# Moving the first expert group's preparation forward into the relu layer of a two-layer transformer kernel

## The reference

```python
x = x + L0_xattn(layernorm(x), ctx)
x = x + L0_ffn(layernorm(x))                    # 8 experts choose tokens, small attention inside
x = x + L1_xattn(layernorm(x), ctx, masks)      # self attention, cross attention, relu FFN
x = x + L1_ffn(layernorm(x))                    # 16 routed experts and 2 shared ones
```

```python
h = relu(y @ ff_w1 + ff_b1)                     # 128 -> 512
y = layernorm(y + h @ ff_w2 + ff_b2, g3, b3)    # divides by (std + EPS)
x = x + y
```

```python
xn = layernorm(x)
scores = sigmoid(xn @ router_w.T); s = scores + bias
# groups of 4 experts: sum of the two best; the best 2 of 4 groups stay
# among what stays the best 4 experts; weights = scores / sum * 2.5
routed = sum_e combine[:, e] * (silu(xn @ gate_w[e]) * (xn @ up_w[e])) @ down_w[e]
shared = silu(xn @ sh_gate_w) * (xn @ sh_up_w) @ sh_down_w
x = x + routed + shared
```

## Time and profile before

| what | us |
|---|---|
| median of 3 runs | 2225.53 |
| lowest and highest run | 2221.91, 2232.56 |
| the profiled execution, its own time | 2221.45 |
| its span in the profile | 2219.7 |
| PE busy | 2008.3 (90%) |
| DVE busy | 1675.7 (75%) |
| ACT busy | 1060.3 (48%) |
| POOL busy | 449.9 (20%) |

### The profile page before, as it was taken

How to read it: one execution, slowest core, us unless ns; L and a number is a source line. 1 busy time by engine, 2 the same in 40 slices (tenths; PEclk the granted TensorE clock), 3 DMA queues, 4 the chain that set the end, 5 groups by cost and what they waited for, 6 DMA issues and landing times. The chain is left out here.

```text
span 2219.7 us, 53046 instructions
## 1 busy us (share of the span) xinstructions
PE 2008.3 (90%) x19268; PEld 1552.4 (70%) x19268; DVE 1675.7 (75%) x4618; ACT 1060.3 (48%) x2084; POOL 449.9 (20%) x504
## 2 busy tenths in 40 slices
PE   7999994878769999996999997987999999999998
PEld 4666663666646666664666665765888888888887
DVE  5777776787646888885888885667888888888886
ACT  5666552545534555552545553553444444444443
POOL 1111100000001323231222222573111111111111
PEclk9999997999978999995999998998999999999999
DMA  3000000000000000000100001000000000000000
GB/s 123 29 28 28 28 1 0 1 1 0 0 1 2 0 0 0 0 0 29 30 28 19 28 19 62 3 1 1 6 11 5 5 5 10 5 5 10 5 5 10
DMA packets 27396, 30.36 MB, mean 14 GB/s; under 512 B 1952, under 2 KB 20640, under 8 KB 27040
## 3 DMA queue, kind: packets, MB, share of 16 engines
q1 hardware_dynamic: 27296, 29.18, 4.1%
HBM read 24.98 MB, written 4.19 MB: 13 GB/s over the span
## 5 line engine op out<-in xcount | busy, mean ns | idle before, releaser
L454 DVE TENSOR_REDUCE mx<-ps 128x8 f32<-128x512 f32 x384 | 262.2, 683 | 176.0 <-PE ps L643 175.8
L361 ACT ACTIVATE ex<-ps 128x512 f32<-128x512 f32 x384 | 230.2, 599 | 271.4 <-PE ps L661 269.6
L1086 ACT ACTIVATE y_res<-ps 128x512 f32<-128x512 f32 x288 | 172.4, 599 | 348.1 <-PE ps L1172 347.9
L1154 PEld LDWEIGHTS ps<-down,y_res 128*128 128x128 f32 x2048 | 267.3, 191 | 23.3 <-issue 1.5
L661 PE MATMUL ps<-pack,sh 128*128 128x128 f32 x1536 | 251.9, 286 | 31.5 <-DVE sh L456 30.8
L456 DVE TENSOR_TENSOR sh<-ps,mx 128x512 f32<-128x512 f32 x384 | 265.6, 692 | 13.2
L1154 PE MATMUL ps<-down,y_res 128*128 128x128 f32 x2048 | 270.0, 275 | 0.8 <-DVE y_res L1432 0.4
L677 PEld LDWEIGHTS ps<-vblk,ex 128*64 128x64 f32 x6144 | 214.0, 139 | 66.0 <-issue 66.0
L1414 DVE TENSOR_TENSOR y_res<-ps,y_res 128x512 f32<-128x512 f32 x288 | 198.1, 688 | 80.3 <-PE ps L1172 67.7
L661 PEld LDWEIGHTS ps<-pack,sh 128*128 128x128 f32 x1536 | 169.8, 142 | 125.9 <-issue 66.2
L677 PE MATMUL ps<-vblk,ex 128*64 128x32 f32 x6144 | 257.0, 227 | 0.0
(11 more groups left out here) (237 smaller groups left out, 3437.6 us busy)
## 6 DMA issues: line engine op xcount, KB each, us to landing
ctxT<-in_ctx SPq DMA_DIRECT2D x32, 256.0 KB, 2.9
x_res<-in_x SPq DMA_DIRECT2D x16, 256.0 KB, 3.0
kmi<-in_key_mask SPq DMA_DIRECT2D x16, 256.0 KB, 3.3
out<-y_res SPq DMA_DIRECT2D x16, 256.0 KB, 2.3
pack<-in_pack SPq DMA_DIRECT2D x1, 2053.0 KB, 10.8
wqkv<-in_wqkv SPq DMA_DIRECT2D x1, 1536.0 KB, 11.0
gate<-in_gate SPq DMA_DIRECT2D x6, 192.0 KB, 4.1
up<-in_up SPq DMA_DIRECT2D x6, 192.0 KB, 4.2
```

Of the source, the lines that this page charges most:

```text
L361: nc.scalar.activation(ex[:, u % 2], UB[u % 4].rearrange("p (c n) -> p c n", n=P), ACT.Exp).then_inc(e_ready, 1)
L454: nc.vector.tensor_reduce(mx[:, u % 2], sc, AX.X, ALU.max).then_inc(max_done, 1)
L1154: last = nc.tensor.matmul(YB[k % 2][:, t * D:(t + 1) * D], act_[:, k % 3, t * P:(t + 1) * P], down[:, k, :], start=True, stop=True)
```

## The change

LOOPED goes from 8 to 4, so that steps 5 to 15 of the relu layer are written out, and everything counted from it moves: the weights are split in steps 5 to 10, and NORM_AT, TURN_AT and LOGITS_AT are steps 9, 10 and 11 where they were 13, 14 and 15. Group 0's routing leaves the expert layer for DVE's relu steps: parts 0 to 2 behind step 12, parts 3 to 5 behind step 13, parts 6 and 7 behind step 14. PE gets two waits, since the relu steps now go on behind `make_xT` and `logits`: step 11 begins when ACT has copied bank 6, step 12 when ACT has read bank 7. `low_rows` on POOL moves from ahead of the last step to behind step 10. On DVE the last step no longer adds step 14's rows to x_res; `first_group` does it behind product 1, and step 15's behind product 4. `norm_stats` and `norm_apply` of group 1 move from behind products 1 and 2 to behind products 2 and 3.

```diff
--- before.py
+++ after.py
@@ -929,7 +929,7 @@
 
 
 
-        LOOPED = 8
+        LOOPED = 4
 
         def relu_steps(eng, prep, step):
             prep(0, 0)
@@ -950,7 +950,8 @@
 
 
         SPLIT_AT = LOOPED + 1
-        NORM_AT, TURN_AT, LOGITS_AT = NG - 3, NG - 2, NG - 1
+        NORM_AT, TURN_AT, LOGITS_AT = 9, 10, 11
+        ROUTE_AT = {12: (0, 1, 2), 13: (3, 4, 5), 14: (6, 7)}
 
         @block.sync
         def _(sp):
@@ -1036,9 +1037,9 @@
 
 
             def r_step_and_more(g, s, first, more):
-                if type(g) is int and g == LOGITS_AT:
+                r_step(g, s, first, more)
+                if type(g) is int and g == TURN_AT:
                     low_rows(0, 0)
-                r_step(g, s, first, more)
                 if type(g) is int and SPLIT_AT <= g < SPLIT_AT + K // CH:
                     split_weights(g - SPLIT_AT)
                 if type(g) is int and g == NORM_AT:
@@ -1222,6 +1223,11 @@
 
 
             def r_step_and_more(g, s, first, more):
+                if type(g) is int and g == TURN_AT + 1:
+
+                    pe.wait_ge(xT_copied, 1)
+                if type(g) is int and g == LOGITS_AT + 1:
+                    pe.wait_ge(exp_done, 1)
                 r_step(g, s, first, more)
                 if type(g) is int and g == TURN_AT:
                     make_xT(0, 0)
@@ -1255,7 +1261,7 @@
                 for t in range(TILES):
                     last = nc.vector.bn_aggr(r_mv[:, t, :], r_st[:, t, :])
                 last.then_inc(r_moments, 1)
-                if not first:
+                if not first and more:
                     add_to_x(g - 1, 1 - s)
                 if more:
                     scale_rows(g)
@@ -1436,11 +1442,11 @@
 
             def first_group(k):
 
-                if k < 4:
-                    route(0, 0, (2 * k, 2 * k + 1))
                 if k == 0:
                     scale_rows(NG - 1)
-                if k == 3:
+                if k == 1:
+                    add_to_x(NG - 2, 0)
+                if k == 4:
                     add_to_x(NG - 1, 1)
 
             ROUTE_SLOTS = (6, 7, 8, 9, 10, 11, 14, 16)
@@ -1454,9 +1460,9 @@
                     product(g, k, first)
                     if first:
                         first_group(k)
-                    if more and k == (1 if first else 0):
+                    if more and k == (2 if first else 0):
                         norm_stats(g + 1, 1 - s)
-                    if more and k == 2:
+                    if more and k == (3 if first else 2):
                         norm_apply(g + 1, 1 - s)
                     for part, at in enumerate(ROUTE_SLOTS):
                         if more and k == at:
@@ -1472,6 +1478,8 @@
                     norm_stats(0, 0)
                 if type(g) is int and g == TURN_AT:
                     norm_apply(0, 0)
+                if type(g) is int and g in ROUTE_AT:
+                    route(0, 0, ROUTE_AT[g])
 
             relu_steps(dve, lambda g, s: None, r_step_and_more)
             expert_steps(dve, step)
```

## The result

The changed kernel takes 2240.78 us (median of 4 runs, 2238.63 to 2243.93), the kernel before 2224.81 (4 runs, 2221.91 to 2232.56). The ratio is 1.0067, 95% interval [1.0039, 1.0096]: slower by about 15 us. The profiled execution has a span of 2241.7 us, 22.0 more than before.

What follows compares the result with a forecast made beforehand. The prediction took time to be lost where PE, busy 90% of the span, stands waiting. Terms 1.4 + 0.5 + 9.2 - 5.0 = +6.1 us gave 2227.5 us for the profiled execution, 2231.5 for a median; range 2220.9 to 2240.

Steps and rivals of the forecast that it cites:

- The hole only moves: PE's 14.60 us wait for group 0's `norm_apply` comes 4 steps earlier, with 1.9 us of lower clock behind it: cost 0.
- Bank 6: PE's step 11 must wait for ACT's second copy, starting 2.27 us behind the transposes instead of 0.91: cost 1.4 us.
- bank 7: PE's step 12 must wait until ACT's exponential behind the logits has ended: cost 0.5 us.
- The routing in steps 12 to 14: Routing plus POOL's hold-ups delay DVE; expert 2 begins at S + 42.1 (S: step 12's start on PE): cost 9.2 us.
- The two bare rows: Two trace rows of routing instructions slowed beside POOL's gain and offset, 0.5 + 0.8 us: alone 1.3 us a step.
- The first group: Without routing between products, expert 2 to expert 10 takes 23.1 us instead of 28.06: a gain of 5.0 us.
- The sum: All terms together, 1.4 + 0.5 + 9.2 - 5.0 = +6.1 us, bounds -4.6 and +11.8.
- Written-out steps instead of looped ones: Relu steps written out rather than looped take PE the same 7.44 us: cost 0.
- The rival of the lower clock: New PE waits leave the clock below full at expert 5 and later, each costing up to 1.9 us; chance 0.16.
- My 2237.3 us: The lower-clock rival's time: +5.7 us on +6.1, over the 2236.7 us bound for slower.
- the upper bound of the local sum: Up to expert 10, routing at its worst and no gain in the first group: 1.9 + 9.9 - 0 = +11.8 us.

Runs made afterwards that it cites:

- Experiment 6: Changed kernel with DVE's expert layer written out and POOL's gain and offset left out in relu steps 12 to 14, for timing alone: 2215.77 us, ratio 0.9966.
- N = 72: Kernel before with 72 extra semaphore increments on DVE ahead of its first relu step, its expert loop then placed as in the changed kernel: 2238.52 us, ratio 1.0081.
- N = 4: Changed kernel with 4 extra semaphore increments on DVE ahead of its first relu step: 2225.85 us, ratio to the kernel before 1.0019.
- N = 120: Changed kernel with 120 extra semaphore increments on DVE ahead of its first relu step: 2235.62 us, ratio to the kernel before 1.0067.

## Why the prediction was right in its parts and wrong in its sum

- **The hole only moves, cost 0**: right, 14.59 us. The step behind it took 9.92 us (1480.47 to the logits at 1490.39) instead of 9.35, so 0.6 us were missing.
- **Bank 6, 1.4 us, and bank 7, 0.5**: right. Step 11 starts 2.28 us behind its transposes, 1.37 more than before (the rows give 1508.70 - 1506.48 = 2.22, not the 2.27 I wrote); step 12 starts 1.27 behind the logits instead of 0.82.
- **The routing in steps 12 to 14, 9.2 us**: 8.1. Step 12 starts at 1491.66 and expert 2 at S + 41.04, forecast S + 42.1. DVE's three steps take 30.5 us, not 31.8. Experiment 6 splits the term: without POOL they take 25.9, and 6.04 + 2.86, 6.04 + 3.13 and 6.04 + 1.86 were 8.90, 9.17 and 7.90 for measured 8.92, 9.19 and 7.77. Only POOL's share was mis-sized, 4.6 us where I took 5.8. The two bare rows, 1.3 a step, would have given 3.9, which is nearer. The Trainium skill's exclusive lock (SBUF — State Buffer, the section on the two separate sides) led me to 5.8; the trace agrees that the lock is there, 1.07 us for 0.19, but not for nearly all of POOL's time. DVE's lateness at steps 13, 14 and 15 is 2.8, 6.2 and 4.9 us, forecast 3, 7 and 6.
- **The first group, -5.0 us**: 23.55 us from expert 2 to 10 instead of 23.1, so -4.5.
- **The sum, +6.1 us up to expert 10**: measured +5.67.
- **"Written-out steps instead of looped ones: PE has the same 7.44 us in both, cost 0"**: this step failed. It looked at the written-out steps and at PE alone. What they cost lies 170 us and more behind them: the four steps push DVE's expert loop 72 instructions on, its head to three instructions ahead of a fetch border, and six jumps back each wait for two blocks. Measured: 14.6 us, where the step had 0. Two runs bear it out (N = 72 in the kernel before adds 15.9, of which 13.9 are not the first group's clock; N = 4 in the changed kernel takes 14.4). The rows were there to be read: before the change the waits view had 2.2 us "<- issue" at the same instruction five times. I never asked what that was, or what would change it. The Trainium skill (Runtime: NRT & Kernel Launch, instruction fetch mechanics) says that a taken branch whose target is outside the fetched window stalls until it is there; the trace agrees, with 2.2 us a fetch.
- **The rival of the lower clock** was not at work. At expert 5 and later the clock is 1.00. Behind each of DVE's doubled stalls it is 0.66 for 5 us, but with N = 72 it is 1.00 there and a turn is only 0.2 us shorter. My 2237.3 us came near the result for a reason that had no part in it.
- **That the time came out within 0.8 us of the range was luck.** The range reached up to 2240 for the clock and for the upper bound of the local sum, and neither happened. The local sum was right; the 14.6 us beside it are more than twice as large, and nothing in the prediction stood for them.

## What to carry to other kernels

When an edit adds or removes instructions ahead of a hardware loop, cost the loop too: look at the first instruction behind its jump back in the trace, for idle time put down to nothing, and at the records of instruction fetches beside it. Before judging any schedule on such a kernel, shift the loop by a few empty instructions, or write it out on that engine; otherwise position (14.5 us here) drowns what is measured (4 to 6 us). Slow products behind a wait are not a cost by themselves: see whether the engine would have waited anyway. And a hole behind a late result can be cheaper to remove than to move: letting PE make the transposes two steps later gave 12.8 us here, more than twice what the change itself cost.

## What the runs showed of the hardware

- On DVE a fetch of instructions took 2.2 us and brought some 8 KB. Each jump back of the loop of 448 instructions paid one, and paid two with its head just ahead of a border (4.34 to 4.67 us, head at 14 modulo 128; 2.20 to 2.24 us at 18 and 70). At 6 it paid the second a dozen instructions later, and with the slow clock behind it that cost as much: 853.65 us against 854.4.
- Straight-line code of DVE, 3667 instructions in all, showed none of these stalls in the expert layer.
- The clock behind PE's short waits can't be told from their length. Over the 4 us behind the wait at a jump back it was 1.00 behind 1.27 us (kernel before), 0.61 to 0.65 behind 1.88 to 2.16 us (changed kernel, all six turns), and 1.00 behind 1.89 to 2.20 us (N = 72, all six). With N = 120 it was 1.00 once, behind 1.99 us, and 0.57 to 0.59 five times, behind 1.92 to 2.22 us. Behind a wait of 3.4 us in the first group it came out either way.
- A DVE instruction of 0.19 us with two inputs took 1.07 us beside a POOL instruction of 128x512, and 0.19 with that left out.
- A semaphore increment cost DVE at most 0.11 us (184 of them in an idle time of 20.51 us).
